# Four-layer attention and expert kernel: the fourth stream's normed rows move from VectorE to GpSimd in two attentions

## What is computed

```
def _layernorm(x, axis=-1, eps=1e-05):
    m = jnp.mean(x, axis=axis, keepdims=True)
    v = jnp.var(x, axis=axis, keepdims=True)
    return (x - m) / jnp.sqrt(v + eps)
...
    x = x + _L1_xattn_ref(_layernorm(x, axis=-1), ctx_1024, L1_xattn_Wq, L1_xattn_bq, L1_xattn_Wk, L1_xattn_bk, L1_xattn_Wv, L1_xattn_bv, L1_xattn_Wp, L1_xattn_bp)
    x = x + _L1_ffn_ref(_layernorm(x, axis=-1), L1_ffn_router_w, L1_ffn_router_b, L1_ffn_W, L1_ffn_V, L1_ffn_W_out)
...
    x = x + _L3_xattn_ref(_layernorm(x, axis=-1), ctx_1024, ctx_1024, mask_BxS2_ik1, L3_xattn_Wq_w, L3_xattn_Wq_b, L3_xattn_Wk_w, L3_xattn_Wk_b)
    x = x + _L3_ffn_ref(_layernorm(x, axis=-1), L3_ffn_gate_w, L3_ffn_w1, L3_ffn_b1, L3_ffn_w2, L3_ffn_b2)
```

## Time and profile before

| | |
|---|---|
| median of 3 runs | 1673.55 us (1666.23 to 1673.93) |
| the profiled execution's own time | 1664.46 us |
| its span, first to last instruction | 1662.6 us |
| mean granted TensorE clock | 0.897 |
| TensorE, VectorE, GpSimd busy | 1398.9, 1121.4, 767.3 us |

### The profile page before, as it was taken

How to read it: one execution, slowest core, us unless ns; L and a number is a source line. 1 busy time by engine, 2 the same in 40 slices (tenths; PEclk the granted TensorE clock), 3 DMA queues, 4 the chain that set the end, 5 groups by cost and what they waited for, 6 DMA issues and landing times. The chain is left out here.

```text
span 1662.6 us, 37562 instructions
## 1 busy us (share of the span) xinstructions
PE 1398.9 (84%) x10866; PEld 1301.8 (78%) x10867; DVE 1121.4 (67%) x3528; ACT 903.6 (54%) x2726; POOL 767.3 (46%) x775
## 2 busy tenths in 40 slices
PE   6687699946877389999999999999998399667398
PEld 4566599945666289999999999999998399545298
DVE  5646755558767367778787877878776466576455
ACT  4354155522323178777778787777775134244254
POOL 4066444420004454556757575757554456303344
PEclk9797899977657699999999999999999699878599
DMA  9201122250220300000000000000000323531322
GB/s 233 34 32 57 52 57 67 64 182 1 103 75 30 123 14 1 14 2 19 10 16 10 7 19 0 25 0 13 1 14 6 107 79 84 164 103 52 115 81 70
DMA packets 88412, 88.70 MB, mean 53 GB/s; under 512 B 17058, under 2 KB 74761, under 8 KB 87927
## 3 DMA queue, kind: packets, MB, share of 16 engines
q1 hardware_dynamic: 72472, 58.20, 12.8%
q0 software_dynamic: 12448, 26.27, 4.6%
q10 hardware_dynamic: 3392, 3.02, 0.7%
HBM read 54.06 MB, written 34.91 MB: 54 GB/s over the span
## 5 line engine op out<-in xcount | busy, mean ns | idle before, releaser
L2130 POOL TENSOR_TENSOR paired_rows<-paired_rows,rinv 128x1024 f32<-128x1024 f32 x128 | 242.7, 1896 | 243.6 <-DVE rinv L2451 228.6
L2442 DVE TENSOR_TENSOR probs_turned_lo<-psum_banks,probs_turned_hi 128x512 fp32r<-128x512 f32 x256 | 175.5, 686 | 137.7 <-ACT probs_turned_hi L2295 133.3
L2321 ACT ACTIVATE paired_rows<-psum_banks,neg_max 128x256 f32<-128x256 f32 x512 | 237.2, 485 | 0.6 <-DVEq L2022 0.4
L2242 PE MATMUL psum_banks<-probs_turned_hi,y_rows 128*128 128x256 f32 x1024 | 214.8, 293 | 0.9 <-DVEq L2022 0.9
L2192 PE MATMUL psum_banks<-y_turned_parts,queries_hi 128*128 128x256 f32 x1024 | 199.6, 293 | 3.0 <-DVEq L2022 3.0
L2242 PEld LDWEIGHTS psum_banks<-probs_turned_hi,y_rows 128*128 128x128 f32 x1024 | 167.5, 190 | 1.7 <-DVEq L2022 1.6
L2295 ACT CAST probs_turned_hi<-psum_banks 128x512 fp32r<-128x512 f32 x256 | 151.2, 591 | 19.9 <-PE psum_banks L2163 8.3
L2192 PEld LDWEIGHTS psum_banks<-y_turned_parts,queries_hi 128*128 128x128 f32 x1024 | 157.7, 190 | 3.6 <-issue 3.6
L2163 PE MATMUL psum_banks<-ident,paired_rows 128*128 128x128 f32 x1024 | 155.5, 274 | 5.3 <-DVE probs_turned_lo L2442 2.9
L2457 DVE TENSOR_REDUCE neg_max<-psum_banks 128x4 f32<-128x1024 f32 x128 | 155.4, 1214 | 3.7 <-PE psum_banks L2192 3.5
L2192 PE MATMUL psum_banks<-y_turned_parts,queries_lo 128*128 128x256 f32 x512 | 145.0, 283 | 0.0
(11 more groups left out here) (721 smaller groups left out, 3787.1 us busy)
## 6 DMA issues: line engine op xcount, KB each, us to landing
paired_rows<-expert_rows SPq DMA_DIRECT2D x16, 512.0 KB, 6.0
expert_w_a<-rows_by_expert_last SPq DMA_DIRECT2D x39, 129.0 KB
tile_rows<-rows_by_expert_first SPq DMA_DIRECT2D x71, 65.0 KB
tile_rows<-rows_by_expert SPq DMA_DIRECT2D x71, 65.0 KB
expert_w_b<-in_L_ffn_w_dram SPq DMA_DIRECT2D x2, 2048.0 KB, 12.6
tile_rows<-expert_rows SPq DMA_DIRECT2D x8, 512.0 KB, 3.7
x_rows<-in_x_dram SPq DMA_DIRECT2D x8, 256.0 KB, 5.4
ctx_turned_dram<-ctx_turned SPq DMA_DIRECT2D x1, 2048.0 KB, 11.1
```

What stands on the lines that cost most here:

```text
L2130: ins = pool.tensor_tensor(probs[:, k, :, :], probs[:, k, :, :], rinv[:, k, :].unsqueeze(2).to_broadcast([P, 4, 256]), ALU.mult)
L2242: ins = pe.matmul(bank[Z_BANK][:, r * 256:(r + 1) * 256], yrows[:, 2 * s1 + y, (2 * r + k) * P:(2 * r + k + 1) * P], probsT[x][:, (u + 1) ...
L2321: ins = act.activation(probs[:, par, h, :], bank[S_BANKS[par] + h // 2][:, (h % 2) * 256:(h % 2 + 1) * 256], ACT.Exp, bias=nmax[:, par, h: ...
L2442: ins = dve.tensor_tensor(lo, bank[bank_][:, :], hi.bitcast(F32), ALU.subtract)
```

## The change

VectorE's norm line writes the rows of streams 0 to 2 only. GpSimd makes those of stream 3, for the four groups of the second attention and the three of the fourth: it waits for a new semaphore `scales_refined`, which VectorE's last refinement of the scales raises, and (in heads) for ScalarE's last copy of the tile's old content, subtracts the mean from all four tiles in one instruction, drains, multiplies by the scale in a second, and raises the stream's VectorE semaphore in VectorE's place. TensorE's and ScalarE's programs stay as they are.

The last block of the diff is the fourth attention's GpSimd program; VectorE's calls of `head_norms` and `tail_norms` change there as in the second.

```
+        scales_refined = counter("scales_refined")
...
-            ch.link(dve.scalar_tensor_tensor(rstd, sq, 1.5, rstd, ALU.add, ALU.mult))
...
+            ins = dve.scalar_tensor_tensor(rstd, sq, 1.5, rstd, ALU.add, ALU.mult)
+            if refined:
+                ins.then_inc(refined.sem, 1)
+            ch.link(ins)
...
-            for w in range(W):
+            scales_by_log(ch, dve, i, tail, st["mv"][:, :, 1], st["rstd"][:, :], st["work"], begun, scales_refined if by_pool else None)
+            for w in range(W - 1 if by_pool else W):
...
+            if by_pool:
+                by_pool()
+
+        def last_stream_norm(pool, n, st, src, dst, signal, free=None):
+            own = slice((W - 1) * G, W * G)
+            pool.wait_ge(scales_refined.sem, scales_refined.value + n)
+            if free:
+                free()
+            pool.tensor_tensor(dst, src, st["mv"][:, own, 0:1].to_broadcast([P, G, P]), ALU.subtract)
+            pool.drain()
+            pool.tensor_tensor(dst, dst, st["rstd"][:, own].unsqueeze(2).to_broadcast([P, G, P]), ALU.mult).then_inc(signal, 1)
...
+                @block.gpsimd
+                def _(pool):
+                    for i in range(TURNS):
+                        own, S = group(X, i * W + W - 1), SS[W - 1]
+                        last_stream_norm(pool, 2 * i + 1, st, own, T[W - 1]["u"][:, :, :], S.dve.sem, lambda: pool.wait_ge(S.act.sem, turn_before(S.ACT, i)))
+                        last_stream_norm(pool, 2 * i + 2, st_tail, own, T[W - 1]["tl"]["rows"][:, :, :], S.dve.sem)
...
-                            head_norms(dve, ch, i, SS, st, T)
+                            head_norms(dve, ch, i, SS, st, T, pooled=True)
...
-                        tail_norms(dve, ch, i, SS, st_tail, T, taken=True)
+                        tail_norms(dve, ch, i, SS, st_tail, T, taken=True, pooled=True)
...
-                            head_norms(dve, ch, i + 1, SS, st, T, True)
+                            head_norms(dve, ch, i + 1, SS, st, T, True, pooled=True)
...
                     pool.tensor_copy(last_pad.bitcast(U32)[:, LAST_TO:LAST_TO + 1], spare_row[:, 0:1]).then_inc(last_pad_made.sem, 1)
+                    S = SS[W - 1]
+                    first, second = ((i * W + W - 1) * G for i in range(TURNS))
+                    last_stream_norm(pool, 1, st, X[:, first:first + G, :], T[W - 1]["u"][:, :, :], S.dve.sem, lambda: pool.wait_ge(S.act.sem, turn_before(S.ACT, 0)))
+                    last_stream_norm(pool, 2, st_tail, LAST_ROWS[:, first:first + G, P:2 * P], T[W - 1]["tl"]["rows"][:, :, :], S.dve.sem)
+                    last_stream_norm(pool, 3, st, X[:, second:second + G, :], T[W - 1]["u"][:, :, :], S.dve.sem, lambda: pool.wait_ge(S.act.sem, turn_before(S.ACT, 1)))
```

More of the change, by code:

```diff
@@ L444, in seed_scales, with refine_scales @@
             ch.link(dve.tensor_scalar(rstd.bitcast(I32), bits, -1.0, RSQRT_SEED, ALU.mult, ALU.add))
-        def refine_scales(ch, dve, rstd, work):
+        def refine_scales(ch, dve, rstd, work, refined=None):
             half, sq = work[:, 0, :], work[:, 1, :]
@@ L450, in refine_scales, with scales_by_log @@
             ch.link(dve.tensor_tensor(sq, sq, half, ALU.mult))
-            ch.link(dve.scalar_tensor_tensor(rstd, sq, 1.5, rstd, ALU.add, ALU.mult))
-        def scales_by_log(ch, dve, i, tail, var, rstd, work, begun=False):
+            ins = dve.scalar_tensor_tensor(rstd, sq, 1.5, rstd, ALU.add, ALU.mult)
+            if refined:
+                ins.then_inc(refined.sem, 1)
+            ch.link(ins)
+        def scales_by_log(ch, dve, i, tail, var, rstd, work, begun=False, refined=None):
             if not begun:
@@ L457, in scales_by_log @@
             dve.wait_ge(roots_made.sem, i * 2 + (roots_made.value + 1 + tail))
-            refine_scales(ch, dve, rstd, work)
+            refine_scales(ch, dve, rstd, work, refined)
         def roots_by_log(act, i, tail, st):
@@ L500, in norm_rows, with head_norms @@
                 signal(w, ins)
-        def head_norms(dve, ch, i, SS, st, T, begun=False):
+            if by_pool:
[8 more added lines that the diff above has]
+            pool.tensor_tensor(dst, dst, st["rstd"][:, own].unsqueeze(2).to_broadcast([P, G, P]), ALU.mult).then_inc(signal, 1)
+        def head_norms(dve, ch, i, SS, st, T, begun=False, pooled=False):
             norm_rows(dve, ch, i, 0, st, lambda w: x_tile(i * W + w), lambda w: tile_in(T[w]["u"]),
                       lambda w, ins: ins.then_inc(SS[w].dve.sem, SS[w].DVE.tick("u_normed")),
-                      lambda w: dve.wait_ge(SS[w].act.sem, turn_before(SS[w].ACT, i)), begun)
+                      lambda w: dve.wait_ge(SS[w].act.sem, turn_before(SS[w].ACT, i)), begun,
+                      (lambda: SS[W - 1].DVE.tick("u_normed")) if pooled else None)
         def begin_scales(dve, ch, st):
@@ L584, in tail_tiles, with tail_norms @@
                     "ix": sb_in(ph, "tail_index", [P, G, E], U32), "lg": sb_in(ph, "tail_logits", [P, G, E])}
-        def tail_norms(dve, ch, i, SS, st, T, taken=False, src=x_tile):
+        def tail_norms(dve, ch, i, SS, st, T, taken=False, src=x_tile, pooled=False):
             if not taken:
@@ L594, in tail_norms @@
             norm_rows(dve, ch, i, 1, st, lambda w: src(i * W + w), lambda w: tile_in(T[w]["tl"]["rows"]),
-                      lambda w, ins: ins.then_inc(SS[w].dve.sem, SS[w].DVE.tick("tail_normed")))
+                      lambda w, ins: ins.then_inc(SS[w].dve.sem, SS[w].DVE.tick("tail_normed")),
+                      by_pool=(lambda: SS[W - 1].DVE.tick("tail_normed")) if pooled else None)
         def tail_dve(dve, ch, g, i, S, tl, logits_bank, hot=None, to=ROWS.bitcast(U32)[:, :, P]):
@@ L1890, in attention_1 @@
                 close_streams(SS)
+                scales_refined.value += 2 * TURNS
                 close_rows(layer_before)
@@ L2811, in _ @@
                         if i < TURNS - 1:
-                            tail_norms(dve, ch, i, SS, st_tail, T, src=last_x)
+                            tail_norms(dve, ch, i, SS, st_tail, T, src=last_x, pooled=True)
                             begin_scales(dve, ch, st)
```

3 lines of the change are left out of this document (1 added, 2 removed).

## The result

The changed kernel takes 1674.19 us, the median of 20 runs, beside 1669.01 us for the kernel before in the 20 runs beside it: ratio 1.0033, 95% interval 1.0019 to 1.0048, so about 5.2 us slower. The forecast was 8.0 us, and 1681.6 us. Of the 7.4 us by which 1681.6 was missed, 4.5 are the base: the three runs shown ahead of the change had a median of 1673.55 us, these twenty 1669.01.

What follows compares the result with a forecast made beforehand. TensorE's end of stream 3's transposes was taken to set the time at six of seven places, VectorE's L2774 at the seventh. Delays of 6.45, 1.0 and 0.57 us gave 8.0 us more, 1681.6 us; range 1669 to 1688.

Steps and rivals of the forecast that it cites:

- The hold: At the seven places, each GpSimd instruction blocks VectorE through shared SBUF ports for 0.8 us, 1.6 us a pair; chance 0.50.
- the last head: Fourth attention's head at 1503.5 us: L2774, and with it stream 3's transpose, comes 0.57 us later.
- The tail at 1489.4: Fourth attention's tail at 1489.4 us, where the clock rises inside stream 3's transposes: 1.0 us later.
- Rival 3: No hold worth the name at the places; TensorE gets stream 3 without a gap: about 3 us faster, 1670.5 us; chance 0.17.
- Rival 2: VectorE keeps GpSimd out at the places, so GpSimd starts 3.1 us in: 7.3 us slower, 1680.9 us; chance 0.15.
- that of the second attention: Second attention's two heads and two tails at the low clock, each 1.29 us later: 5.2 us.
- rival 4: TensorE idles longer ahead of each place and its clock rises later: 3 to 6 us more, 1685 to 1688; chance 0.15.
- The fourth attention's 2.9 us: Fourth attention's three places, 1.29 + 1.0 + 0.57 us later, together 2.9 us.
- Added: 14 GpSimd instructions: At the seven places, a GpSimd pair with its drain takes 2.23 us, as in the third attention.

Runs made afterwards that it cites:

- experiment 4: Changed kernel with a GpSimd drain at the start of the second attention, and GpSimd's subtract and its drain made twice at each place: 1682.11 us, one run.
- experiment 5: Changed kernel with a GpSimd drain at the start of the second attention, GpSimd making only two of stream 3's four tiles: 1669.26 us, one run.
- experiment 9: Kernel before with ScalarE making stream 3's rows at the seven places and one GpSimd drain at the start of the second attention: 1665.73 us, ratio 0.9970.
- experiment 1: Changed kernel with one GpSimd drain added at the start of the second attention: 1673.85 us, ratio 1.0016 to the kernel before.
- experiment 2: Kernel before with one GpSimd drain added at the start of the second attention: 1663.38 us, ratio 0.9965.
- experiment 10: Repeat of experiment 2, the kernel before with one early GpSimd drain: 1665.21 us, ratio 0.9964.
- experiment 12: Repeat of experiment 1, the changed kernel with one early GpSimd drain: 1673.47 us, ratio 1.0024 to the kernel before.
- experiment 7: Kernel before with two GpSimd drains added, at the start of the second attention and behind the last scatter of experts 1: 1667.45 us, ratio 0.9989.
- experiment 8: Kernel before with the two drains of experiment 7 and ScalarE making stream 3's rows at the seven places: 1665.04 us, ratio 0.9972.

## Why the prediction was wrong

- *The hold.* Right in mechanism and close in size. A pair costs VectorE 0.77 + 0.72 = 1.49 us (predicted 1.6), streams 0 to 2 end at 4.65 us (4.8), and GpSimd is done first, at all places but the first head; TensorE's weight loads for stream 3 end at 6.27 us (6.3) at five of them. In the last head they start 0.46 us later than before (0.57), and end 0.75 us later, since they run at the low clock there (0.71 us instead of 0.42). The tail at 1489.4, forecast 1.0 us later, ended 1.4 us later, also at the low clock. Experiments 4 and 5 show it by adding and by shortening; experiment 9 shows that it is GpSimd's. Rival 3, with no hold, is out. The Trainium skill, page "SBUF — State Buffer", section "Who interferes with whom", has the loser blocked for the whole instruction. The rows agree on the hold, but it is 0.27 to 0.37 us less than the full length. Rival 2 is out: GpSimd started with VectorE and kept its 1.04 and 1.09 us.
- *The sum of it.* 8.0 us predicted; experiments 1, 2, 10 and 12 have 8.5 and 10.0 us with the drain out of the way, and the runs can't tell these from 8.0. In the profiled executions the term that was too small is that of the second attention, 5.2 us for what measured 7.4: the prediction kept the clock apart as rival 4, whole or not at all, where a part of it came. Two lost pieces of 3 us each at the high level go with it; rival 4's 3 to 6 us did not come. The fourth attention's 2.9 us are neither shown nor excluded.
- *The step that failed.* "Added: 14 GpSimd instructions", priced by the pair of the third attention at 2.23 us with its drain. That drain stands behind no transfers. The one in the first head stands behind the 71 scatters of experts 0 (and the 64 of the first attention), took 7.94 us, of which 1.1 are the wait for the subtract as at the other places, and held up TensorE's stream 3 until 9.1 us behind the first rows instead of 5.4, a stall worth between nothing and 3.5 us by the runs. By the same move the drain that opens the third attention, which TensorE waits for, fell from 9.35 us to 2.88. The prediction looked for what the change adds at its own places and took the program elsewhere as unmoved, though the wait of 16.95 us for GpSimd at 570 us, with a drain of 9.35 us in it, stood in the trace. That second part alone is worth 5.9 us on the kernel before (0.9965 and 0.9964).
- *The balance.* 8.5 to 10.0 us of hold and clock, less 5.9 us at the third attention, and 0 to 3.5 us for the stall: 2.6 to 7.6 us, measured 5.2 and (1.0022) 3.7 us. The lower end is no check of its own: it is the ratio of experiment 1 by another way. What the forecast of 8.0 us lacked is a gain that has nothing to do with the rows. That its 1681.6 us and the measured 1674.19 both lie in 1669 to 1688 is luck: the range was made for other causes.
- *What stays open.* The trace of experiment 2 shows 5.2 us gained by the second group of the third attention, but that whole stretch was only 337.3 - 334.3 = 3.0 us shorter, and in experiment 10 1.5 us, at a lower granted clock (0.93 against 0.94); over ten profiled executions with the short drain there (all but experiments 7 and 8) it took 332.1 to 336.9 us, 333.8 on average, against 337.3 and 337.4 in the two with the long one, so about 3.6 us less. That fits the 3.8 us of the trace better than the measured 5.9 us (intervals together 2.0 to 9.8); how these divide between the place and the clock is not settled. Nor is why a drain takes time for transfers that have landed, and by what count; only that it does. And the worth of the stall by itself lies within the spread of the clock.

The version that beats both kernels is the kernel before with one drain on GpSimd at the start of the second attention: 0.9965 and 0.9964.

## What to carry to other kernels

Work moved from VectorE to GpSimd beside VectorE's own stream is not parallel: two GpSimd instructions of 1.04 and 1.09 us took 1.49 us from VectorE, to save it 1.03; ScalarE took the same rows without stretching a tile of VectorE's. Before putting a drain on an engine that issues indirect transfers, count the transfers since its last one, back to the start of the program if need be, and where a drain on the path is long, put one earlier, where the engine idles and nothing waits for it. When an added instruction carries such a side effect, look at the next place where that engine is waited for, even if it is two phases away.

## What the runs showed of the hardware

- A GpSimd drain behind indirect transfers took 2.67 and 2.87 us for 32 of them since the last drain, 2.91 for 35, 7.50 for 87 and 8.25 for 100 (0.08 to 0.09 us each), but 6.85 for 135 and 9.35 for 167. It is no wait for data: with 100, the last packet had ended 7.2 us before the drain did.
- Beside a GpSimd TENSOR_TENSOR of 1.04 us a VectorE TENSOR_SCALAR of 128x128 took 1105 to 1109 ns instead of 340, beside one of 1.09 us 1055 to 1059 ns, and 678 ns beside one of 0.61 us. The others of the same stream ran at 333 ns, slightly quicker than before. GpSimd lost at most 0.05 us (1.04 and 1.09 us, against 1.05 and 1.04 for its like in the earlier trace rows).
- A ScalarE Identity of 128x128 with scale and bias from SBUF took 480 ns and left VectorE at 340 ns.
